# A whole copy of the experts' weights beside their two parts, and one product in place of two for the last 32 tokens

## The chip, the cores and the metric

One core of one Trainium2 chip. The time is the device time of one execution, in microseconds. The kernel before was run three times; the median is 1820.77 us, with 1818.58 and 1825.10 as the ends. Lines (L1254) are lines of the kernel before.

## The reference

The kernel computes one metaformer layer over 64 images of 128 channels and 28 x 28 pixels, in fp32. A first half gates each image by position and by channel. The second half is a mixture of experts over tokens, and the change lies there:

```python
router_probs = jax.nn.softmax(x @ router_w + router_b, axis=-1)
top_p, top_i = jax.lax.top_k(router_probs, K)                  # K = 2 of E = 8 experts
top_p = top_p / jnp.sum(top_p, axis=-1, keepdims=True)
expert_out = jnp.einsum('bnd,edc->bnec', x, expert_w) + expert_b
gathered = jnp.take_along_axis(expert_out, top_i[..., None], axis=2)
return jnp.einsum('bnk,bnkc->bnc', top_p, gathered)
```

Here x is a token's 128 channels after a normalisation, and the result is added to the token.

## The kernel before

**Work and tiles.** Two images make a pair; there are 32 pairs, one after the other. A pair has 1568 tokens: twelve tiles of 128 and a rest of 32. All eight experts are computed for every token, and the gates, 0 for all but two, weigh them. TensorE (PE) multiplies, ACT gates experts 0 to 3 into `part` (`gate_low`, L809), VectorE (DVE) adds experts 4 to 7 (`gate_high`, L1695), GpSimd (POOL) adds the four partial sums into `otok` (`add_token`, L570 and L575).

**The two parts of a number.** The products of the full tiles are made in the faster fp32r form. The centred tokens `cen` are cut into `xh` (rounded, by ACT, `x_high`) and `xl` (what is left, by POOL, `x_low`, L545), the weights into `weh` and `wel`. Three products with 512 columns (L1247 to L1249) make one half of the experts for a tile. The rest of 32 tokens is handled on its own in `rest_products` (L1254): a full fp32 product of `cen` with `weh` and then one with `wel`, each for four pairs of experts. The four write to four groups of 32 rows of one PSUM buffer. Both operands are taken as fp32.

**Where the weights come from.** The experts' weights arrive once by DMA in `raw_we`, a view on the buffer `part`, which is not used for its own purpose before. PE makes their mean, DVE subtracts it in place, ACT copies to `weh`, DVE subtracts that to make `wel`.

**Order.** Each engine runs a list of steps written out by hand. One step takes work of five pairs at different stages; the number behind a call says how many pairs back. On PE the stretch around the changed work is

```python
channels(1, 3)
rstd_turn(1)
logits(4)
low_half(0, 4)        # rest_products
gram_first(3)
router(4)
low_half(1, 4)
gram_turn(3)
finish(3, 5)
channels(2, 3)
joint_c(3)
joint(0, 1, 2)
hidden_c(3)
high_half(1, 4)
```

and later `low_half(2, 4)`, `low_half(3, 4)`, `high_half(3, 4)`. Semaphores tie the engines together: `gram_first` waits for ACT's second group of `chan` (L753), `router` for ACT's copy of the logits (L791), DVE's `route_first` (L1644 to L1658, with `pick` at L1634 to L1637) for `router`, `joint(0, 1)` (L1057) for the PSUM bank that DVE's `finish(3)` (L1705) empties, `high_half(3)` (L1247) for `gate_high(1)` (L1695). ACT and DVE gate by `gv` (L1680), the last step of the routing. POOL's list has `x_low(0)`, `add_token(12)`, `x_low(1)`, `x_low(2)`, `x_low(3)` in this stretch. The DMA queue (SP) stores results, loads images and spreads rows of numbers over all partitions (`y_ch` from `rstd_rows`).

Of the kernel before, what the change touches and what calls it, by code (L numbers as in the profile page):

```python
# [5 lines left out]
ALU = mybir.AluOpType  # L6
ACT = mybir.ActivationFunctionType
F32 = mybir.dt.float32
F32R = mybir.dt.float32r
BF16 = mybir.dt.bfloat16  # L10
AX_X = mybir.AxisListType.X


BATCH, C, HH, WW = 64, 128, 28, 28
S = HH * WW
# [3 lines left out]
E = 8  # L19
PAIR = 2  # L20
# [9 lines left out]
BIG = 1e30  # L30
# [53 lines left out]
TILES = -(-PAIR * S // 128)  # L84
# [27 lines left out]
def metaformer_kernel(nc, a, out):  # L112
    with ExitStack() as ctx:
        def sb(name, shape, dt=F32):
            return ctx.enter_context(nc.sbuf_tensor(name, shape, dt))
# [3 lines left out]
        def sem(name):  # L119
            if name not in sems:  # L120
                sems[name] = ctx.enter_context(nc.semaphore(name))
            return sems[name]
# [30 lines left out]
        pref = sb("pref", [128, E])  # L153
        weh = sb("weh", [C, E, C], F32R)
        wel = sb("wel", [C, E, C], F32R)
        mhalf = sb("mhalf", [128, 2 * NT])


# [2 lines left out]
        cen = sb("cen", [C, PAIR, S])  # L161
# [38 lines left out]
        cg = sb("cg", [C, PAIR])  # L200
        logit = sb("logit", [128, 416])
        lg = sb("lg", [128, TILES, E])
        lg2 = sb("lg2", [128, TILES, E])
        eq = sb("eq", [128, TILES, E])
        first = sb("first", [128, TILES, E])
        second = sb("second", [128, TILES, E])
        mx = sb("mx", [128, 8, TILES])
# [12 lines left out]
        def live(k, p, back):  # L220

            return not isinstance(k, int) or 0 <= 2 * k + p - back < UNITS
# [23 lines left out]
        def need(eng, name, k, p, n, back):  # L246

            if isinstance(k, int) and 2 * k + p - back < 0:
                return
            eng.wait_ge(sem(name), k * (2 * PER[name]) + ((p - back) * PER[name] + n))  # L250

        def rows(i):

            return min(128, PAIR * S - 128 * i)
# [5 lines left out]
        def flat(v):  # L260

            return v[:, :, :].rearrange("p b s -> p (b s)")
# [21 lines left out]
        def bank(use, k, p, back):  # L284

            return rot[((2 * k + p - back + USES[INDEX[use]][1]) * NU + INDEX[use]) % NB]
# [26 lines left out]
        room = part[:, :, :, :].rearrange("p r e c -> p (r e c)")  # L313
# [13 lines left out]
        pad_wc1 = spare[0:DC, 7 * C:10 * C].rearrange("p (t c) -> p t c", t=3)  # L327
        raw_swc1 = scrap[0:DC, 12:13]
        raw_sbc = scrap[:, 13:15]
        raw_we = room[:, 0:E * C].rearrange("p (e c) -> p e c", e=E)  # L330
        avg = scrap[:, 128:256]
        neg_avg = scrap[0:1, 256:384]
        raw_wr = scrap[:, 64:64 + E]
# [563 lines left out]
        def _(pe):  # L897
# [65 lines left out]
            def step(pe, k, p, ahead=False):  # L963
# [285 lines left out]
                    return nc.tensor.matmul(dst[:, :], flat(xl[o])[:, cols_t], hi_w, start=False, stop=True)  # L1249

                def rest_products(dst):
                    for n, w in enumerate((weh, wel)):
                        for g in range(4):
                            last = nc.tensor.matmul(dst[32 * g:32 * g + 32, 0:2 * C], flat(cen)[:, 128 * (TILES - 1):PAIR * S],  # L1254
                                                    w[:, 2 * g:2 * g + 2, :].rearrange("p e c -> p (e c)").bitcast(F32),
                                                    start=(n == 0), stop=(n == 1))
                    return last

                def tile_ready(t, back):
# [4 lines left out]
                def low_half(i, back):  # L1264
                    if live(k, p, back):
                        if opening(k, p, back):
                            pe.wait_ge(sem("weh_ready"), 1)
                            pe.wait_ge(sem("weights_ready"), 1)
                        m, mb = ago(i, 2, back)
                        need(pe, "low_gated", k, p, m + 1, mb)  # L1270
                        if m == 0:
                            need(pe, "high_gated", k, p, 1, mb)
                        dst = low[count_of(k, p, back, i) % 2]
                        if i == 0:
                            need(pe, "centred_ready", k, p, 4, back)
                            rest_products(dst).then_inc(sem("low_filled"), 1)
                        else:
                            tile_ready(tile(i), back)
                            products(dst, tile(i), slice(0, HALF), back).then_inc(sem("low_filled"), 1)
# [108 lines left out]
        def _(dve):  # L1388
# [9 lines left out]
            for e in range(E):  # L1398
                last = nc.vector.memset(pref[:, e:e + 1], float(E - e))
# [77 lines left out]
            def step(dve, k, p, ahead=False):  # L1477
# [5 lines left out]
                def then(ins, name, back):  # L1483

                    count[0] += 1
                    ins.then_inc(sem(name), 1)
                    need(dve, name, k, p, count[0], back)
# [135 lines left out]
                def tiles(v):  # L1623
                    return v.unsqueeze(2).to_broadcast([128, TILES, E])

                def each(v):
                    return v.unsqueeze(1).to_broadcast([128, TILES, E])

                def line(v):
                    return v[:, :, :].rearrange("p i e -> p (i e)")  # L1630

                def pick(logits, top, hot, back):

                    then(nc.vector.tensor_tensor(eq[:, :, :], logits[:, :, :], tiles(top), ALU.is_equal), "route", back)  # L1634
                    then(nc.vector.tensor_tensor(eq[:, :, :], eq[:, :, :], each(pref[:, :]), ALU.mult), "route", back)
                    then(nc.vector.tensor_reduce(mx[:, 4, :], eq[:, :, :], AX_X, ALU.max), "route", back)
                    then(nc.vector.tensor_tensor(hot[:, :, :], eq[:, :, :], tiles(mx[:, 4, :]), ALU.is_equal), "route", back)  # L1637

                def route_first(back):
                    if live(k, p, back):  # L1640
                        count[0] = 0
                        need(dve, "rlogit_filled", k, p, 1, back)
                        src = bank("rlogit", k, p, back)
                        nc.vector.tensor_tensor(lg[:, 0:12, :].rearrange("p (g t) e -> p g t e", t=3),  # L1644
                                                src[:, 0:384].rearrange("p (t g e) -> p g t e", t=3, g=4)[:, :, :, 0:E],
                                                rstd2[:, 0:12].rearrange("p (g t) -> p g t", t=3).unsqueeze(3)
                                                .to_broadcast([128, 4, 3, E]), ALU.mult)
                        n = rows(12)
                        last = nc.vector.tensor_tensor(lg[0:n, 12, :], src[0:n, 480:480 + E],
                                                       rstd2[0:n, 12:13].to_broadcast([n, E]), ALU.mult)  # L1650
                        last.then_inc(sem("rlogit_read"), 1)
                        need(dve, "rlogit_read", k, p, 1, back)
                        then(nc.vector.tensor_reduce(mx[:, 0, :], lg[:, :, :], AX_X, ALU.max), "route", back)
                        pick(lg, mx[:, 0, :], first, back)
                        then(nc.vector.scalar_tensor_tensor(out=line(lg2), in0=line(first), scalar=-BIG, in1=line(lg),
                                                            op0=ALU.mult, op1=ALU.add), "route", back)
                        then(nc.vector.tensor_reduce(mx[:, 1, :], lg2[:, :, :], AX_X, ALU.max), "route", back)
                        nc.vector.tensor_tensor(mx[:, 2, :], mx[:, 1, :], mx[:, 0, :], ALU.subtract)\  # L1658
                            .then_inc(sem("rgap_ready"), 1)
                        assert count[0] == 7  # L1660

                def route_second(back):
                    if live(k, p, back):
                        count[0] = 7
                        pick(lg2, mx[:, 1, :], second, back)
                        assert count[0] == 11

                def route_gates(back):
# [82 lines left out]
                centre_tokens(1, 1)  # L1751
                finish(2, 5)
                route_first(4)
                finish(3, 5)
                route_second(4)
                route_gates(4)
                normalise(0, 0, 1)
# [46 lines left out]
```

## Time and profile before

| | |
|---|---|
| three runs, median (ends) | 1820.77 us (1818.58 to 1825.10) |
| the profiled execution, its time | 1818.09 us |
| its span, first to last instruction | 1816.3 us |
| mean granted TensorE clock | 0.99 |
| busy, share of the span | PE 96%, DVE 79%, ACT 67%, POOL 62% |
| one pair in steady work, from first rest product to the next pair's | 53.4 to 53.7 us |
| L1254 | 512 records of PE |

A record of PE is one pass of a matmul; an fp32 product has two, so that eight products for a pair are 16 records. The timeline merges successive instructions of one kind into one row, with the start of the first and the time until the end of the last. Ends of matmuls are modelled, since they overlap: starts are the surer numbers. An idle time stands in brackets, with what ended it.

### The profile page before, as it was taken

The numbers are of one execution on the slowest core, as the hardware profiler recorded it, in microseconds if no ns is written. First come the engines' busy times: TensorE is split into PE (matmuls) and PEld (weight loads), VectorE is DVE, ScalarE is ACT, GpSimd is POOL, SyncE is SP. The second block draws the span as 40 slices with busy tenths as digits, with TensorE's granted clock in tenths as the row PEclk, the third lists the DMA queues.
The fourth block names the chain that finished last, engine by engine and source line by source line (L and its number), as shares of the span: only waits on it lengthen the run. The fifth ranks groups of instructions, "written<-read, shape, count | busy, mean of one in ns | idle before, by whom it ended". The sixth has DMA issues, their size and how long they took to land.

```text
span 1816.3 us, 39474 instructions
## 1 busy us (share of the span) xinstructions
PE 1748.9 (96%) x13396; PEld 1295.2 (71%) x13396; DVE 1434.1 (79%) x4703; ACT 1210.0 (67%) x3346; POOL 1132.6 (62%) x1268
## 2 busy tenths in 40 slices
PE   4789999999999999999999999999999999999996
PEld 2467777777777777777777777777777777777774
DVE  4467888888888888888888888888888888887666
ACT  4447667677666667666767776666776676776554
POOL 1135666766667676666767666767666676766565
PEclk9799999999999999999999999999999999999998
DMA  4122222112222211222211222221122221121111
GB/s 136 37 73 72 73 90 75 70 63 82 73 90 90 73 64 63 90 72 90 83 62 64 81 73 90 90 73 63 64 90 72 90 90 60 62 78 65 44 55 54
DMA packets 56181, 135.18 MB, mean 74 GB/s; under 512 B 16268, under 2 KB 18333, under 8 KB 55982
## 3 DMA queue, kind: packets, MB, share of 16 engines
q1 hardware_dynamic: 55320, 130.81, 20.8%
q8 instruction: 110, 1.80, 0.4%
q10 hardware_dynamic: 662, 1.84, 0.4%
q14 instruction: 89, 0.73, 0.1%
HBM read 106.50 MB, written 26.13 MB: 73 GB/s over the span
## 4 chain that ended last, share of the span: by engine, by line
PE 92%; DVE 3%; ACT 2%; DMA 1%; issue 1%; POOL 1%; SPq 0%; POOLq 0%; ACTq 0%; DVEq 0%
PE rot L1101 6%; PE rot L1111 6%; PE rot L1102 6%; PE low L1247 5%; PE high L1247 5%; PE rot L1057 5%; PE low L1249 5%; PE low L1248 5%; PE high L1249 5%; PE high L1248 5%; PE rot L1037 4%; PE rot L1070 3%; PE rot L1238 3%; PE rot L981 3%; PE rot L1004 3%; PE rot L1200 3%
## 5 line engine op out<-in xcount | busy, mean ns | idle before, releaser
L809 ACT ACTIVATE part<-low,gv 128x128 f32<-128x128 f32 (+1 forms) x1664 | 475.2, 376 | 166.9 <-PE low L1249 89.4
L570 POOL TENSOR_TENSOR part<-part 128x256 f32<-128x256 f32 (+1 forms) x416 | 331.4, 797 | 327.3 <-DVE part L1695 321.5
L1695 DVE SCALAR_TENSOR_TENSOR part<-high,gv,part 128x128 f32<-128x128 f32 x1536 | 424.7, 342 | 81.3 <-ACT part L809 47.7
L575 POOL TENSOR_TENSOR otok<-part 128x128 f32<-128x128 f32 (+1 forms) x416 | 263.5, 633 | 32.6
L1101 PE MATMUL rot<-x1h,wch 128*128 128x256 f32 x960 | 237.3, 286 | 0.0
L1102 PE MATMUL rot<-x1h,wcl 128*128 128x256 f32 x960 | 230.9, 280 | 0.0
L535 POOL TENSOR_TENSOR tp_l<-tp,tp_h 128x448 fp32r<-128x448 f32 x64 | 65.6, 1024 | 239.4 <-ACT tp_h L686 239.3
L1101 PEld LDWEIGHTS rot<-x1h,wch 128*128 128x128 f32 x960 | 181.4, 189 | 3.5 <-issue 0.9
L1102 PEld LDWEIGHTS rot<-x1h,wcl 128*128 128x128 f32 x960 | 181.9, 189 | 1.3
L1247 PE MATMUL low<-weh,xh 128*128 128x512 f32 x384 | 170.2, 443 | 7.8 <-DVE part L1695 7.5
L703 ACT ACTIVATE j<-rot,bggs 128x448 f32<-128x448 f32 (+3 forms) x256 | 136.1, 582 | 58.5 <-PE rot L1057 55.6
L1247 PE MATMUL high<-weh,xh 128*128 128x512 f32 x384 | 163.7, 426 | 2.7 <-DVE part L1695 2.6
L1249 PE MATMUL low<-weh,xl 128*128 128x512 f32 x384 | 152.1, 396 | 0.0
L1249 PE MATMUL high<-weh,xl 128*128 128x512 f32 x384 | 151.8, 395 | 0.0
L1248 PE MATMUL low<-wel,xh 128*128 128x512 f32 x384 | 151.7, 395 | 0.0
L1248 PE MATMUL high<-wel,xh 128*128 128x512 f32 x384 | 151.1, 394 | 0.0
L554 POOL TENSOR_TENSOR x1l<-tok,x1h 128x1024 fp32r<-128x1024 f32 x64 | 117.7, 1838 | 33.6 <-ACT x1h L741 32.7
L1111 PE MATMUL rot<-x1l,wch 128*128 128x256 f32 x960 | 137.6, 279 | 0.5 <-POOL x1h L559 0.5
L545 POOL TENSOR_TENSOR xl<-cen,xh 128x384 fp32r<-128x384 f32 x128 | 127.1, 1015 | 2.7 <-ACT xh L786 2.7
L1111 PEld LDWEIGHTS rot<-x1l,wch 128*128 128x128 f32 x960 | 125.4, 189 | 3.2 <-POOL x1h L559 0.7
L753 ACT ACTIVATE chan<-rot,bc 128x256 f32<-128x256 f32 x160 | 68.7, 470 | 69.2 <-PE rot L1113 69.1
L1644 DVE TENSOR_TENSOR lg<-rot,rstd 128x96 f32<-128x96 f32 x32 | 8.2, 258 | 132.7 <-PE rot L1228 132.7
(247 smaller groups left out, 3995.3 us busy)
## 6 DMA issues: line engine op xcount, KB each, us to landing
xin<-in_x SPq DMA_DIRECT2D x32, 784.0 KB, 4.4
x<-in_x SPq DMA_DIRECT2D x32, 784.0 KB, 4.3
cen<-shift_rows SPq DMA_DIRECT2D x32, 784.0 KB, 4.0
out<-x SPq DMA_DIRECT2D x64, 392.0 KB, 2.4
y_ch<-rstd_rows SPq DMA_DIRECT2D x32, 768.0 KB, 3.8
otok<-in_ggs_w SPq DMA_DIRECT2D x1, 600.2 KB
tok<-in_ggs_w SPq DMA_DIRECT2D x1, 600.2 KB
rstd_rows<-both_rows SPq DMA_DIRECT2D x32, 7.0 KB
```

What stands on the lines that cost most here:

```text
L545: nc.gpsimd.tensor_tensor(flat(xl[o])[:, own], flat(cen)[:, own], flat(xh[o])[:, own].bitcast(F32), ALU.subtract)\
L570: nc.gpsimd.tensor_tensor(part[0:n, slot, 0:2, :], part[0:n, slot, 0:2, :], part[0:n, slot, 2:4, :], ALU.add).then_inc(sem("half_sum"), 1)
L575: nc.gpsimd.tensor_tensor(otok[0:n, t, :], part[0:n, slot, 0, :], part[0:n, slot, 1, :], ALU.add).then_inc(sem("token_ready"), 1)
L703: nc.scalar.activation((j1, j2)[m][0:rows, b, cols(q)], bank(f"joint{b}{q}{m}", k, p, back)[0:rows, 0:width(q)], ACT.Relu, bias=bggs[0:row ...
L809: last = nc.scalar.activation(part[0:n, turn % RING, e, :], src, ACT.Copy, scale=gv[par(p, back)][0:n, t, e:e + 1])
L1101: nc.tensor.matmul(dst, wch[:, j, rows], hi_x, start=(j == 0), stop=False)
L1102: nc.tensor.matmul(dst, wcl[:, j, rows], hi_x, start=False, stop=False)
L1111: nc.tensor.matmul(dst, wch[:, j, rows], x1l[:, j, :, :].rearrange("p b c -> p (b c)"), start=False, stop=False)
L1247: nc.tensor.matmul(dst[:, :], flat(xh[o])[:, cols_t], hi_w, start=True, stop=False)
L1248: nc.tensor.matmul(dst[:, :], flat(xh[o])[:, cols_t], lo_w, start=False, stop=False)
L1249: return nc.tensor.matmul(dst[:, :], flat(xl[o])[:, cols_t], hi_w, start=False, stop=True)
L1695: last = nc.vector.scalar_tensor_tensor(out=own, in0=src, scalar=gv[par(p, back)][0:n, t, HALF + e:HALF + e + 1], in1=own, op0=ALU.mult, o ...
```

## The change

The whole weights get a buffer of their own, `we`, and stay there after the two parts are made. The rest of 32 tokens takes one full fp32 product with `we` for each pair of experts, where it took one with `weh` and one with `wel`. To make room, `lg2`, the router's logits with the first choice masked out, is given up, and the masked logits are written over `lg`. `raw_we` becomes another name for `we`; the lines that load, centre and cut the weights are the same.

```diff
         wel = sb("wel", [C, E, C], F32R)
+        we = sb("we", [C, E, C])
...
-        lg2 = sb("lg2", [128, TILES, E])
...
-        raw_we = room[:, 0:E * C].rearrange("p (e c) -> p e c", e=E)
+        raw_we = we[:, :, :]
...
                 def rest_products(dst):
-                    for n, w in enumerate((weh, wel)):
-                        for g in range(4):
-                            last = nc.tensor.matmul(dst[32 * g:32 * g + 32, 0:2 * C], flat(cen)[:, 128 * (TILES - 1):PAIR * S],
-                                                    w[:, 2 * g:2 * g + 2, :].rearrange("p e c -> p (e c)").bitcast(F32),
-                                                    start=(n == 0), stop=(n == 1))
+                    for g in range(4):
+                        last = nc.tensor.matmul(dst[32 * g:32 * g + 32, 0:2 * C], flat(cen)[:, 128 * (TILES - 1):PAIR * S],
+                                                we[:, 2 * g:2 * g + 2, :].rearrange("p e c -> p (e c)"), start=True, stop=True)
                     return last
...
-                        then(nc.vector.scalar_tensor_tensor(out=line(lg2), in0=line(first), scalar=-BIG, in1=line(lg),
+                        then(nc.vector.scalar_tensor_tensor(out=line(lg), in0=line(first), scalar=-BIG, in1=line(lg),
                                                             op0=ALU.mult, op1=ALU.add), "route", back)
-                        then(nc.vector.tensor_reduce(mx[:, 1, :], lg2[:, :, :], AX_X, ALU.max), "route", back)
+                        then(nc.vector.tensor_reduce(mx[:, 1, :], lg[:, :, :], AX_X, ALU.max), "route", back)
...
-                        pick(lg2, mx[:, 1, :], second, back)
+                        pick(lg, mx[:, 1, :], second, back)
```

## Rows read from the trace of the kernel before

**Rows 1.** Busy us (instructions) of each engine in a stretch, clock, DMA share, GB/s.
```profile
900.00:1200.00 300.00, 300.00 (x2318) 221.50 (x2317) 250.07 (x825) 212.97 (x590) 197.11 (x219) 1.00 0.22 77
```
**Rows 2.** Timeline of PE, pair at 943.6: start, us, engine, line, what, count.
```profile
943.56 0.61 PE L1254 MATMUL low<-weh,cen 128*32 128x256 f32 x8
944.00 0.61 PE L1254 MATMUL low<-wel,cen 128*32 128x256 f32 x8
944.54 1.16 PE L1145 MATMUL rot<-chan 128*128 128x128 f32 x8
945.53 0.60 PE L1228 MATMUL rot<-ident,logit 128*128 128x128 f32 x4
```
**Rows 3.** Line L1254: count, ns least/median/most, first and last start.
```profile
L1254 PE MATMUL low<-wel,cen x256: 379/379/634, 141.4 to 1779.7; 128*32 128x256 f32 x128
```
**Rows 4.** Timeline of ACT, pair at 943.6.
```profile
942.84 0.84 ACT L753 ACTIVATE chan<-rot,bc 128x256 f32<-128x256 f32 x2 [1.55 <-PE rot L1113]
...
943.81 0.51 ACT L791 COPY logit<-rot 128x416 f32<-128x416 f32 x1
```
**Rows 5.** Timeline of DVE, pair at 997.0.
```profile
1000.24 0.72 DVE L1634 TENSOR_TENSOR eq<-lg,mx 128x104 f32<-128x104 f32 x1
1001.00 0.96 DVE L1635 TENSOR_TENSOR eq<-eq,pref 128x104 f32<-128x104 f32 x1
...
1002.28 0.27 DVE L1637 TENSOR_TENSOR first<-eq,mx 128x104 f32<-128x104 f32 x1
...
1003.27 0.58 DVE L1705 TENSOR_TENSOR x<-rot,x 128x416 f32<-128x416 f32 x1
```
**Rows 6.** Timeline of POOL, pair at 997.0: second and third `x_low` of the row.
```profile
999.83 1.01 POOL L545 TENSOR_TENSOR xl<-cen,xh 128x384 fp32r<-128x384 f32 x1
...
1000.79 1.04 POOL L545 TENSOR_TENSOR xl<-cen,xh 128x384 fp32r<-128x384 f32 x1
```
**Rows 7.** Timeline of DVE, pair at 943.6.
```profile
946.82 0.58 DVE L1634 TENSOR_TENSOR eq<-lg,mx 128x104 f32<-128x104 f32 x1
...
949.72 0.58 DVE L1705 TENSOR_TENSOR x<-rot,x 128x416 f32<-128x416 f32 x1
```
**Rows 8.** Timeline of POOL, pair at 943.6: the `x_low` in the middle.
```profile
946.28 1.00 POOL L545 TENSOR_TENSOR xl<-cen,xh 128x384 fp32r<-128x384 f32 x1
```
**Rows 9.** Timeline of DVE, pair at 836.5.
```profile
839.73 0.40 DVE L1634 TENSOR_TENSOR eq<-lg,mx 128x104 f32<-128x104 f32 x1
...
841.44 0.67 DVE L1637 TENSOR_TENSOR first<-eq,mx 128x104 f32<-128x104 f32 x1
```
**Rows 10.** Timeline of POOL, pair at 836.5: three `x_low` back to back.
```profile
838.99 3.00 POOL L545 TENSOR_TENSOR xl<-cen,xh 128x384 fp32r<-128x384 f32 x3
```
**Rows 11.** Timeline of DVE, moments of the pair behind, at 932.8.
```profile
932.78 0.18 DVE L1496 TENSOR_TENSOR sm<-st 128x14 f32<-128x14 f32 x1
932.88 0.73 DVE L1497 TENSOR_TENSOR sm<-st 128x14 f32<-128x14 f32 x1
```
**Rows 12.** Timeline of POOL at the same time.
```profile
932.77 0.79 POOL L570 TENSOR_TENSOR part<-part 128x256 f32<-128x256 f32 x1
```
**Rows 13.** Timeline of PE: `joint(0,1)` of two pairs, `high_half(3)` of one.
```profile
950.48 0.42 PE L1057 MATMUL rot<-tp_h,mix_h 64*68 64x448 f32 x2
...
1003.83 0.49 PE L1057 MATMUL rot<-tp_h,mix_h 64*68 64x448 f32 x2
...
1011.51 0.39 PE L1247 MATMUL high<-weh,xh 128*128 128x512 f32 x1
```
**Rows 14.** Timeline of DVE, pair at 997.0: `gate_high(1)`.
```profile
1010.05 1.12 DVE L1695 SCALAR_TENSOR_TENSOR part<-high,gv,part 128x128 f32<-128x128 f32 x4
```
**Rows 15.** Timeline of PE, last pair: `low_half(2)`.
```profile
1790.99 0.77 PE L1247 MATMUL low<-weh,xh 128*128 128x512 f32 x1 [6.39 <-DVE part L1695]
```
**Rows 16.** Waits of all engines: who for whom, us in all, times, longest.
```profile
DVE y_ch L1525 <- DMA y_ch<-rstd_rows: 15.0, 2, 10.6
```

## Prediction

> **What bounds the kernel now.** I read the busy time by stretch first. In 300 us of steady work TensorE (PE) is busy for all 300, VectorE (DVE) for 250, ACT for 213, GpSimd (POOL) for 197, at full clock [rows 1]. So PE sets the pace, and PE time that goes should come back as time, unless something released by another engine is late. The timeline of PE round the changed line comes second, for the price; the timelines of DVE, POOL and ACT behind it come third, for what is late next. The reader is to see that PE never stands idle for long, but that twice in each pair of images it arrives less than 0.1 us behind DVE. That makes this a question of margins.
>
> **What goes.** Per pair, four fp32 products with `weh` (16 records of PE in all for both weights) start at 943.56, four with `wel` at 944.00, and the next work at 944.54 [rows 2]. One set of four, with its weight loads, is a step of 0.44 us (0.43 by the unrounded starts; 0.54 is the step that includes the change to other work, and it stays). The line has 256 records for `wel`, two for each product, 379 ns almost everywhere, from the first pair to the last [rows 3]: 32 pairs. Were nothing else to wait, the change is worth 32 x 0.43 = 13.8 us.
>
> **What is added or moved.** `we` is another tensor that receives the same DMA as before and is centred by the same instructions; the ACT copy and the DVE subtraction that make `weh` and `wel` are unchanged, once each. No queue gets or loses a transfer. The routing writes its masked logits back into `lg` in place of `lg2`: same instruction, same shape, on an engine that runs in order, so 0. The tensors behind `we` lie 4 KB further on per partition; no row shows a price for a place, and I take 0 both ways. The work that begins 0.43 earlier is the real edit.
>
> **Who meets PE early.** Four things begin before the removed step and are needed behind it. (a) `gram_first` needs ACT's chan copies, which end at 943.68 [rows 4]; PE would come at 944.11. Free. (b) The router's transposes need the logit copy, ended 944.32 [rows 4]; PE would come at 945.10. Free. (c) The spread rstd rows: DVE waited for that transfer twice in the whole run, at most 10.6 us, both at the start [rows 16]. Free. (d) POOL's `x_low`, three instructions back to back, not released by PE here. DVE's routing starts when PE's router transposes end, so it moves 0.43 earlier, and POOL's three do not. These two engines block each other, and here the gain is decided.
>
> In the pair at 997 (call it kind 1) DVE starts L1634 at 1000.24 and takes 0.72, L1635 takes 0.96, and the later L1637 0.27 [rows 5]; undisturbed each takes 0.27. POOL's instructions end at 1000.84 and 1001.83 [rows 6], and DVE's two end 0.12 and 0.13 after them. So a DVE instruction with two SBUF inputs waits out the POOL instruction in flight, and gets in between two. The end of the routing hangs on POOL's third `x_low`, not on PE. Behind it come `finish(3)` (L1705), for which PE waits in `joint(0,1)` (L1057), the gates, and `gate_high(1)` (L1695), for which PE waits in `high_half(3)`. Margins: L1705 ends at 1003.85 [rows 5] and PE is at L1057 from 1003.83 [rows 13], none; L1695 ends at 1011.17 [rows 14], and PE starts 0.34 later [rows 13], about what its release takes. If DVE does not come earlier, PE gains nothing here.
>
> Does it? **Kind 1**: L1634 would come at 999.81. POOL's second `x_low` starts at 999.83 [rows 6]. Rows show the edge elsewhere: L1496 started 0.01 after a POOL instruction and ran its normal 0.18; L1497, 0.11 after the same start, was held, 0.73 [rows 11, 12]. So 0.02 ahead should get in. Then L1635 waits for the second `x_low` instead of the third, L1637 for the third, and it ends near 1001.95 in place of 1002.55: 0.60 earlier, or 0.33 if POOL is meanwhile put off by one DVE instruction (0.27). The bounds of the edge are 0 (missed) and 0.60; I take the hit, being nearer to the row of L1496, and at least 0.43 of it. PE then gains its 0.43 and some 0.02 of today's waits: 0.45. By the length of L1634 and whether L1637 is held, 14 of the 32 pairs are of this kind.
> **Kind 2** (the pair at 943.6; 8 of 32): L1634 starts at 946.82, takes 0.58; POOL's instruction runs from 946.28 [rows 7, 8]. It would come at 946.39, 0.11 after POOL's start, like the L1497 that was held. DVE ends when it did. L1705 ends at 950.30 [rows 7], PE was at L1057 at 950.48 [rows 13] and would be at 950.05: it waits until some 950.35, so 0.13 stays.
> **Kind 3** (the pair at 836; 6 of 32): POOL runs from 838.99 for 3.00, and L1637 too is held, until 842.11, 0.12 behind the last `x_low` [rows 9, 10]. Coming 0.43 earlier changes none of these ends: 0.
> The other four: in the first pair and in the one at 1692 DVE is not held: 0.43 each. In the last two PE waits for DVE anyway (6.39 us in the last, [rows 15]) and DVE would run into POOL: 0.
>
> Sum: 14 x 0.45 + 8 x 0.13 + 6 x 0 + 2 x 0.43 = 6.3 + 1.0 + 0.9 = **8.2 us**. The profiled execution took 1818.1 (span 1816.3), so 1809.9; the median of the runs shown is 1820.8, 2.7 above it, and I forecast against that: **1812.5 us**.
>
> The Trainium skill ("SBUF — State Buffer", section "Who interferes with whom") says that a DVE instruction with two SBUF inputs contends with a GpSimd instruction that reads SBUF, and that whoever issues first keeps the port for its whole instruction. The rows of kind 1 to 3 agree, except that L1496, 0.01 late, was not held. By the strict rule the sum stays 8.2 as long as L1634 is the first by those 0.02 us, and is 1.9 if it is not.
>
> **Rivals.**
> (1) Full gain. The kinds are not fixed: each pair of kind 2 or 3 is followed by one of kind 1. If kind 1 settles in, every pair gives 0.43: 13.8 us, 1807. The distances of successive pairs scatter from 53.4 to 53.7 (table of the profile); if they all came to the lower end, 0.1 or so per pair would be added, 3 us: 1804. For it: PE's 300 of 300. Against: the missing margin at L1057.
> (2) Nothing to speak of. The edge at 999.83 is missed: kind 1 gives 0, the sum is 8 x 0.13 + 2 x 0.43 = 1.9, 1819. For it: 0.02 us is a margin that a small shift of POOL's instructions undoes. It is also what remains if DVE's next instructions are held one POOL instruction longer. That eight products stay is excluded: the loop over the two parts is gone.
> (3) Slower. An earlier DVE instruction that gets in holds POOL back (POOL's L570 took 0.79 in [rows 12] beside DVE). If the third `x_low` ends later by one DVE instruction, 0.27, the routing ends later, and PE, with no margin at L1057, loses 0.27 against today in each of 28 pairs: 7.6 us, 1828. It decides from the point where L1705 ends more than about 0.1 us after PE's present arrival at L1057. Against it: POOL held by 0.27 would have to come with no DVE gain.
>
> **Numbers.** Forecast (gain 5.5 to 11 us) 0.42; full gain (more than 11) 0.28; nothing (within 5.5 us either way) 0.23; slower 0.07. A measurement here can tell some 0.3%, 5.5 us, from no change. Faster 0.70, same 0.23, slower 0.07. The range goes from just under the lower end of (1), 1803.5, to the time of (2) with half a microsecond, 1819.5; the forecast alone would have 1810 to 1815.
>
> **What would show it.** The changed line has 256 records of PE, none with `wel`, and the step from the last logit product to `gram_first` falls from 0.98 to 0.55: price right. The router's transposes follow the first rest product after 1.54, not 1.97 [rows 2]. L1634 of 0.27 where it was 0.72: the edge was hit; of 1.0: missed. If L1705 ends less than 0.1 before the second product of `joint(0,1)` in most pairs, PE's time went into that wait. Wrong I am if kinds other than these turn up, if PE shows new waits before `gram_first` or the router, or if the distance between pairs falls by 0.43 everywhere: then the margins did not matter.

## The result, and the profile after

The changed kernel takes 1818.68 us (median of 20 runs, 1815.81 to 1822.48), the kernel before 1822.66 in 20 runs on the same chip (1818.42 to 1825.10). The ratio is 0.9981, 95% interval 0.9973 to 0.9989: some 3.5 us faster (2.0 to 4.9), where 8.2 were forecast. It is less than the 0.3% that the prediction set as what can be told from no change. The profiled execution took 1818.96.

The work that was to go has gone, at its price. First the source line of the rest products in the trace of after (count, ns least/median/most, first and last start), then PE's timeline in the pair that begins at 945.5 (a pair is named by the start of its first logits, L1218):

```profile
L1253 PE MATMUL low<-we,cen x256: 379/379/634, 145.1 to 1780.8; 128*32 128x256 f32 x128
```
```profile
945.50 0.91 PE L1218 MATMUL rot<-cen,wr 128*32 128x416 f32 x8
946.22 0.61 PE L1253 MATMUL low<-we,cen 128*32 128x256 f32 x8
946.77 1.16 PE L1145 MATMUL rot<-chan 128*128 128x128 f32 x8
947.76 0.60 PE L1228 MATMUL rot<-ident,logit 128*128 128x128 f32 x4
...
952.65 0.77 PE L1057 MATMUL rot<-tp_h,mix_h 64*68 64x448 f32 x2
```

256 records in place of 512 [rows 3]. `gram_first` (L1145) stands 0.55 behind the first rest product and the router's transposes (L1228) 1.54; they stood 0.98 and 1.97 behind it [rows 2]. So PE is 0.43 us earlier at the router in each pair. But the row of L1057 covers 0.77 us for two records, where it was 0.42 [rows 13]: the second of them, which needs the PSUM bank that `finish(3)` empties, waits. Records merge in that view; where the wait is long enough the trace breaks them, as in the pair at 998.8, and names DVE's `finish(3)` (L1703 now, L1705 before; lines behind the change have numbers smaller by two):

```profile
1005.95 0.42 PE L1057 MATMUL rot<-tp_h,mix_h 64*68 64x448 f32 x1
1006.63 0.42 PE L1057 MATMUL rot<-tp_h,mix_h 64*68 64x448 f32 x1 [0.26 <-DVE x L1703]
```

DVE's routing in a pair that was to be of kind 1, at 1213.0. First DVE, then POOL's second and third `x_low` of the row, both of after:

```profile
1216.57 1.09 DVE L1632 TENSOR_TENSOR eq<-lg,mx 128x104 f32<-128x104 f32 x1
1217.69 0.97 DVE L1633 TENSOR_TENSOR eq<-eq,pref 128x104 f32<-128x104 f32 x1
1218.69 0.26 DVE L1634 TENSOR_REDUCE mx<-eq 128x13 f32<-128x104 f32 x1
1218.99 0.27 DVE L1635 TENSOR_TENSOR first<-eq,mx 128x104 f32<-128x104 f32 x1
...
1219.98 0.58 DVE L1703 TENSOR_TENSOR x<-rot,x 128x416 f32<-128x416 f32 x1
```
```profile
1216.54 0.99 POOL L545 TENSOR_TENSOR xl<-cen,xh 128x384 fp32r<-128x384 f32 x1
...
1217.50 1.04 POOL L545 TENSOR_TENSOR xl<-cen,xh 128x384 fp32r<-128x384 f32 x1
```

The first step of `pick` (L1632 now) starts at 1216.57, 0.03 behind POOL's `x_low` at 1216.54, and takes 1.09: held to the end of that instruction, and the next one for 0.97 to the end of the one behind it. In the pair at 997 before, the same two took 0.72 and 0.96 [rows 5]. DVE came 0.43 earlier and was held 0.38 longer, so that `finish(3)` starts 6.96 us behind the pair's first logits (1213.02), before 7.02 (1003.27 [rows 5] less that pair's 996.25). The table of groups says it for the whole run (after; its busy time and mean ns):

```profile
L1632 DVE TENSOR_TENSOR eq<-lg,mx 128x104 f32<-128x104 f32 x64 | 37.4, 585 | 1.1
```
and the same of before:
```profile
L1634 DVE TENSOR_TENSOR eq<-lg,mx 128x104 f32<-128x104 f32 x64 | 26.7, 417 | 1.1
```

These are 10.7 us more in 64 instructions that do the same work. On the page of after DVE is busy for 1445.2 us (1434.1 before), and the chain that ended last passes more through it:

```profile
PE 1747.8 (96%) x13140; PEld 1287.8 (71%) x13140; DVE 1445.2 (80%) x4703; ACT 1206.8 (66%) x3346; POOL 1131.4 (62%) x1268
PE 88%; DVE 7%; ACT 2%; issue 1%; DMA 1%; POOL 1%; SPq 0%; POOLq 0%; ACTq 0%; DVEq 0%
```

Before, that chain had 92% PE and 3% DVE. PE is busy for 1.1 us less of the run, not 13.8: a wait that the modelled ends of the records cover is no idle time there, such as that of the second record of L1057, which starts at 953.00 where the first is shown until 953.07.

**Distance between pairs.** The time from one pair's first logits (L1218) to the next's is the measure used from here on, since what lies ahead of the first pair moved by 4 us between the two profiled executions (first logits at 140.2 before and 144.4 after), whatever the change. From the third pair to the 29th, 26 distances, PE's timeline of after:

```profile
250.17 0.91 PE L1218 MATMUL rot<-cen,wr 128*32 128x416 f32 x8
...
1640.66 0.91 PE L1218 MATMUL rot<-cen,wr 128*32 128x416 f32 x8
```
and of before:
```profile
246.55 0.91 PE L1218 MATMUL rot<-cen,wr 128*32 128x416 f32 x8
...
1638.77 0.91 PE L1218 MATMUL rot<-cen,wr 128*32 128x416 f32 x8
```

1390.49 / 26 = 53.48 and 1392.22 / 26 = 53.55: the change is worth 0.07 us for a pair, where PE's work is 0.43 shorter. With the first two and the last four pairs it makes 3.3 us (1676.1 from first logits to end before, 1672.8 after), which is the measured difference.

### The profile page after: what moved, and what is told of

Read it like the earlier page. It is cut to its first block, busy times and chain, and to the rows that moved or that the text cites. A ratio compares the mean times of both kernels' runs of the same rounds, so it can differ in the third digit from the quotient of the medians.

```text
span 1817.2 us, 38962 instructions
## 1 busy us (share of the span) xinstructions
PE 1747.8 (96%) x13140; PEld 1287.8 (71%) x13140; DVE 1445.2 (80%) x4703; ACT 1206.8 (66%) x3346; POOL 1131.4 (62%) x1268
## 4 chain that ended last, share of the span: by engine, by line
PE 88%; DVE 7%; ACT 2%; issue 1%; DMA 1%; POOL 1%; SPq 0%; POOLq 0%; ACTq 0%; DVEq 0%
PE rot L1101 6%; PE rot L1111 5%; PE rot L1102 5%; PE rot L1057 5%; PE high L1247 5%; PE low L1247 5%; PE high L1249 5%; PE high L1248 5%; PE low L1249 5%; PE low L1248 4%; PE rot L1037 4%; PE rot L1070 3%; PE rot L981 3%; PE rot L1004 3%; PE rot L1200 3%; PE rot L971 2%
## 5 line engine op out<-in xcount | busy, mean ns | idle before, releaser
L570 POOL TENSOR_TENSOR part<-part 128x256 f32<-128x256 f32 (+1 forms) x416 | 328.6, 790 | 324.8 <-DVE part L1693 319.0
L1247 PE MATMUL low<-weh,xh 128*128 128x512 f32 x384 | 169.8, 442 | 8.5 <-DVE part L1693 8.2
L1247 PE MATMUL high<-weh,xh 128*128 128x512 f32 x384 | 163.7, 426 | 2.7 <-DVE part L1693 2.6
L517 POOL TENSOR_TENSOR rstd<-var,mhalf 128x14 f32<-128x14 f32 x32 | 91.1, 2846 | 25.4 <-DVE var L1502 25.2
```

The costliest lines, as they stand in the source:

```text
L570: nc.gpsimd.tensor_tensor(part[0:n, slot, 0:2, :], part[0:n, slot, 0:2, :], part[0:n, slot, 2:4, :], ALU.add).then_inc(sem("half_sum"), 1)
L1247: nc.tensor.matmul(dst[:, :], flat(xh[o])[:, cols_t], hi_w, start=True, stop=False)
```

## Experiments

Two theories stood after the result. **The lock**: DVE's routing is earlier by 0.43, but POOL's two last `x_low` hold it, so `finish(3)` ends when it did, and PE, now early, waits for its bank. **The rival**: the change brings a cost of its own (the place of `we`, the routing writing over `lg`), or the eight products were never worth 0.43 because something hid them. Each line is the median time, the ratio to the kernel before measured beside it, its 95% interval and the mean distance, as above (53.55 before, 53.48 after).

| kernel | us | ratio | distance |
|---|---|---|---|
| a_router | 1821.25 | 0.9991 (0.9980 to 1.0002) | 53.49 |
| b_router | 1834.97 | 1.0073 (1.0059 to 1.0088) | 53.96 |
| a_xlow | 1810.41 | 0.9933 (0.9919 to 0.9948) | 53.04 |
| b_xlow | 1821.55 | 0.9994 (0.9983 to 1.0006) | 53.48 |
| a_two | 1821.35 | 1.0004 (0.9995 to 1.0012) | 53.55 |
| a_nudge | 1812.46 | 0.9961 (0.9946 to 0.9975) | 53.33 |
| a_xlow3 | 1807.20 | 0.9924 (0.9911 to 0.9937) | 53.08 |
| a_banks | 1814.53 | 0.9967 (0.9954 to 0.9979) | 53.28 |
| b_xlow3 | 1821.25 | 0.9996 (0.9985 to 1.0008) | 53.50 |
| b_banks | 1823.40 | 1.0009 (0.9996 to 1.0022) | 53.56 |
| a_xlow3_banks | 1810.03 | 0.9931 (0.9914 to 0.9948) | 53.12 |

a_ kernels are made from the changed kernel, b_ from the one before.

### The routing out of the lock: a_xlow, b_xlow

```diff
                 x_low(1, 4)
-                x_low(2, 4)
-                x_low(3, 4)
                 add_token(0, 4)
 ...
                 add_token(4, 4)
+                x_low(2, 4)
+                x_low(3, 4)
```

> The changed kernel with POOL's x_low(2) and x_low(3) moved behind add_token(4), away from DVE's routing; PE's order is untouched. Theory: L1634, L1635 and L1637 take 0.27 us each except where x_low(1) meets the first, L1705 ends well before PE reaches joint(0,1), distance about 53.0 us, ratio 0.992, if the later xl and token sums make no wait of their own. Rival: as before the move, ratio 0.997 to 0.999.

> The kernel before with the same move of x_low(2) and x_low(3). Theory: distance of pairs about 53.4 us, ratio 0.998, so that the difference to the changed kernel with this move is the price of the products, 0.43 us a pair, some 12 us. Rival: the difference is some 3 us.

Measured: 0.9933, as expected, and 0.9994, where 0.998 was expected. In a_xlow only `x_low(1)` can still meet the routing (in nine pairs it holds the first step, for 0.83 to 0.95 us in all, which costs nothing). In the pair at 992.5 nothing of POOL lies beside it, and DVE's timeline reads

```profile
996.07 0.27 DVE L1632 TENSOR_TENSOR eq<-lg,mx 128x104 f32<-128x104 f32 x1
996.37 0.27 DVE L1633 TENSOR_TENSOR eq<-eq,pref 128x104 f32<-128x104 f32 x1
...
997.96 0.58 DVE L1703 TENSOR_TENSOR x<-rot,x 128x416 f32<-128x416 f32 x1
```

The same instructions take 0.27 in place of 1.09 and 0.97. Between the two kernels, which differ by the whole change, lie 0.43 us for each pair (53.48 - 53.04): its full price. The same move on the kernel before is worth 0.07. There the routing ended about when PE needed it, so the hold cost next to nothing; the change made the hold the bound.

### One move is enough: a_xlow3, b_xlow3

Only `x_low(3)` is moved behind `add_token(4)`.

> The changed kernel with only POOL's x_low(3) moved behind add_token(4). Theory: L1634 is still held by x_low(2), to about 4.6 us behind the logits, but L1635 and L1637 are free; L1705 ends at about 6.5, before PE reaches joint(0,1) at 7.13, so that the whole price comes back: distance 53.0 us, ratio 0.993, as with both moved. Rival (it is the sum of what POOL takes from DVE, so that half the move gives half): distance 53.25, ratio 0.996.

> The kernel before (eight products, lg2) with only POOL's last x_low of the row moved behind the additions to the tokens. Theory (before the change DVE's held routing ended about when PE needed it, so PE was the bound and freeing DVE is worth next to nothing; the change makes PE earlier, and only then does the hold cost): ratio to the kernel before 0.998 to 1.001, mean distance between pairs 53.45 to 53.55 us, and the same edit on the changed kernel is 0.7% ahead of it, 0.43 us for each pair. Rival (the moved x_low is worth its 0.4% on any kernel, and the eight products fewer are worth only 0.2% beside it): ratio 0.995 to 0.996, distance near 53.25.

Measured: 0.9924 and 0.9996, distances 0.41 apart. DVE, POOL (its `x_low(1)` and `x_low(2)` in one row) and PE of a_xlow3, pair at 992.3:

```profile
995.82 1.10 DVE L1632 TENSOR_TENSOR eq<-lg,mx 128x104 f32<-128x104 f32 x1
996.95 0.27 DVE L1633 TENSOR_TENSOR eq<-eq,pref 128x104 f32<-128x104 f32 x1
...
998.54 0.58 DVE L1703 TENSOR_TENSOR x<-rot,x 128x416 f32<-128x416 f32 x1
```
```profile
994.83 1.97 POOL L545 TENSOR_TENSOR xl<-cen,xh 128x384 fp32r<-128x384 f32 x2
```
```profile
999.40 0.42 PE L1057 MATMUL rot<-tp_h,mix_h 64*68 64x448 f32 x2
```

The first step is still held, for 1.10, to 0.12 behind POOL's end at 996.80; the second no longer is. `finish(3)` ends at 999.12, before PE comes to L1057 at 999.40, and the two records of L1057 take 0.42 as before. It is the third `x_low`, and not the hold of the first step, that costs the gain. This is the lowest ratio found, 0.76% ahead of the kernel before; its interval overlaps with those of a_xlow and a_xlow3_banks.

### Later by a tenth on POOL: a_nudge

A tiny instruction of POOL (99 ns, a memory set of a buffer that nothing reads then) is put ahead of `x_low(1)`, so that POOL comes later and DVE first. The line that names its semaphore is left out here.

```diff
                 add_token(12, 5)
+                if live(k, p, 4):
+                    need(pool, "pad_set", k, p, 1, 5)
+                    nc.gpsimd.memset(valid[:, :], 0.0).then_inc(sem("pad_set"), 1)
                 x_low(1, 4)
```

> The changed kernel with one tiny added POOL instruction (a memset of the 128x1 tile valid, which is no longer needed then) ahead of x_low(1), so that POOL's three x_low start a little later, by perhaps 0.1 to 0.3 us. Theory: L1634, which now comes 0.02 to 0.13 us after the start of x_low(2) and is held for 1.1 us, comes while x_low(1) still runs and gets in ahead of x_low(2); L1635 and L1637 are then held by x_low(2) and x_low(3), the routing ends 0.3 to 0.6 us sooner, and the distance falls from 53.48 by 0.1 to 0.35 us: more POOL work, yet 3 to 9 us faster than the changed kernel, ratio 0.993 to 0.997 against before. Rival (the x_low delay PE or DVE by their length, not by where they start): the distance grows or stays, ratio 0.998 or more.

Measured: 0.9961, by the ratios 3.6 us faster than the changed kernel, with an instruction more in each pair; the two intervals touch, but the distance fell from 53.48 to 53.33. Its lines stand three lower. POOL and DVE in the pair at 994.2:

```profile
996.73 0.10 POOL L598 MEMSET valid<- 128x1 f32 x1
...
997.75 1.12 POOL L545 TENSOR_TENSOR xl<-cen,xh 128x384 fp32r<-128x384 f32 x1
```
```profile
997.74 0.27 DVE L1635 TENSOR_TENSOR eq<-lg,mx 128x104 f32<-128x104 f32 x1
998.04 0.95 DVE L1636 TENSOR_TENSOR eq<-eq,pref 128x104 f32<-128x104 f32 x1
...
999.33 0.67 DVE L1638 TENSOR_TENSOR first<-eq,mx 128x104 f32<-128x104 f32 x1
...
1000.72 0.58 DVE L1706 TENSOR_TENSOR x<-rot,x 128x416 f32<-128x416 f32 x1
```

This is kind 1 as the prediction had it: DVE, 0.016 ahead of the second `x_low`, takes 0.27 and stretches it to 1.12; the next step waits for the second and not the third, the later one for the third. From this pair's first logits to the next's are 53.15 us, 0.46 less than the 53.61 of kind 1 before, and 0.45 was the forecast for a hit. The added instruction does not do this everywhere. Where the second `x_low` started 0.09 or more ahead of DVE, the hold stayed; three pairs that took 53.56 to 53.59 in after (357.3, 891.9, 1213.0) now have POOL's row later by 0.8 and take 53.80 to 53.84, while two of 53.80 take 53.15. What is measured is the balance.

### The bank: a_banks, b_banks, a_xlow3_banks

The second product of `joint(0, 1)` takes the bank that ACT's channel copies free, and not the one of `finish(3)`; ACT's `router_exp` moves behind `joint_c(3)`.

```diff
-    ("fin3", 5, "out_ready", 4),
     ("chan2", 3, "chan_ready", 3),
+    ("fin3", 5, "out_ready", 4),
 ...
-                router_exp(4)
                 channels(2, 3)
                 joint_c(3)
+                router_exp(4)
```

> The changed kernel in which joint(0,1) no longer waits for DVE: fin3 and chan2 change places in the rotation of PSUM banks, and ACT does router_exp behind joint_c. POOL's list is untouched, so the routing stays late. Theory: the wait at the second product of joint(0,1) goes, but PE meets the same lateness at low_half(2) or high_half(3), whose gates hang on gate_high(1): distance 53.4 to 53.5 us, ratio 0.997 to 0.998, hardly better than the change alone. Rival (the bank is the whole reason): distance 53.0 us, ratio 0.993.

> The kernel before with the two PSUM banks exchanged, so that the second product of joint(0, 1) takes the bank that ACT's channel copies free and not the one that finish(3) frees. Theory (before the change no wait for finish(3) stood there): ratio 0.999 to 1.001, distance 53.5 to 53.6 us. Rival (the exchange was worth its 0.2% by itself): ratio 0.997 to 0.998, distance near 53.35.

> The changed kernel with both edits: last x_low moved and banks exchanged. Theory (both edits remove the same wait of PE, the one for finish(3), so the second finds nothing left): as with the moved x_low alone, ratio 0.991 to 0.994, distance 53.05 to 53.15 us. Rival (two different losses, which add up): ratio 0.989 to 0.990, distance near 52.9.

Measured: 0.9967, 1.0009 and 0.9931. The ratio of a_banks is close to what the theory had (0.997 to 0.998), but its distance of 53.28 lies below the 53.4 to 53.5 of the theory and above the 53.0 of the rival: the bank is more than half of the loss, not all. PE of a_banks, pair at 945.6:

```profile
952.70 0.49 PE L1057 MATMUL rot<-tp_h,mix_h 64*68 64x448 f32 x2
```

The wait at L1057 is gone (0.49 for two records, 0.77 in after), which shows that it was the wait for `finish(3)`. But only part of the price comes back: 0.20 us a pair more than in after, 0.27 of 0.43 in all. A routing that ends late is then waited for further on: DVE's `gate_high(1)` and PE's `high_half(3)` behind it, in the pair at 892.3 of a_banks:

```profile
906.87 0.34 DVE L1693 SCALAR_TENSOR_TENSOR part<-high,gv,part 128x128 f32<-128x128 f32 x1
```
```profile
906.91 0.39 PE L1249 MATMUL low<-weh,xl 128*128 128x512 f32 x1
907.26 0.50 PE L1247 MATMUL high<-weh,xh 128*128 128x512 f32 x1
```

PE starts 0.05 behind the end of the gate, where it had been 0.34 before [rows 13, 14]. The step to it is 0.35 and its first record 0.50; in after the same step is 0.23 and the record 0.39. So 0.23 us are lost here when the bank doesn't bind first. From the third pair to the 28th it is so in 20 of 26, and the mean over the 26 is 0.15, which is what is missing of the 0.43. On the kernel before the exchange is worth nothing, and beside the moved `x_low` it adds nothing either (0.9931 and 0.9924, intervals overlapping): both remove the same loss.

### What the change itself costs: a_two

The changed kernel with its buffer and its writing over `lg`, but the eight products with `weh` and `wel` put back.

```diff
-                    for g in range(4):
+                    for n, w in enumerate((weh, wel)):
+                        for g in range(4):
 ...
-                                                we[:, 2 * g:2 * g + 2, :].rearrange("p e c -> p (e c)"), start=True, stop=True)
+                                                    w[:, 2 * g:2 * g + 2, :].rearrange("p e c -> p (e c)").bitcast(F32),
+                                                    start=(n == 0), stop=(n == 1))
```

> The changed kernel with the rest's two products put back (weh and wel, eight products), while we keeps its own buffer and the masked logits are still written over lg. Both theories of the wait expect the time of the kernel before, ratio 1.000 within 0.001, distance of pairs 53.5 to 53.6 us. If the new buffer or the write over lg cost something that hid a gain, it shows here as a ratio above 1.001, up to the 10 us that are missing (1.005).

Measured: 1.0004 (0.9995 to 1.0012), distance 53.55. The buffer and the reuse cost nothing that can be seen; the rival falls.

### The router first: a_router, b_router

```diff
                 logits(4)
-                low_half(0, 4)
                 gram_first(3)
                 router(4)
+                low_half(0, 4)
```

> The changed kernel with the rest's product moved on PE behind gram_first and router, so that the router's transposes come 0.54 us sooner behind the logits. Theory (the routing on DVE ends with POOL's last x_low, and PE waits for it at joint(0,1)): DVE's first pick starts 0.54 earlier, gets in one x_low earlier, L1637 ends about 0.6 earlier, the wait at the second product of joint(0,1) (0.35 us and more in every pair of the changed kernel) goes, and the distance of pairs falls from 53.48 to about 53.0 us: some 15 us under the kernel before, ratio 0.992. Rival (the 0.43 us are given back at some other wait, so that DVE's routing is not what holds PE): distance stays near 53.4 to 53.5, ratio 0.997 to 0.999.

> The kernel before with the same move of the rest's eight products behind gram_first and router. Theory: DVE starts 0.98 us sooner, the small waits at joint(0,1) go, the distance of pairs falls from 53.55 to 53.4 us, some 4 us in all, ratio 0.998; the difference to the same move in the changed kernel is then the products' price, 0.43 us a pair, some 12 us. Rival: the difference between the two is some 3 us, as between the kernels without the move.

Measured: 0.9991 and 1.0073, where the theory had 0.992 and 0.998: both missed. DVE's routing starts earlier and the wait at L1057 is gone (0.42 for its two records at 952.10), as hoped, but no time is won. PE of a_router, and ACT's copies of `chan` at the same time:

```profile
944.50 0.91 PE L1218 MATMUL rot<-cen,wr 128*32 128x416 f32 x8
945.48 1.13 PE L1145 MATMUL rot<-chan 128*128 128x128 f32 x8
946.45 0.60 PE L1228 MATMUL rot<-ident,logit 128*128 128x128 f32 x4
946.98 0.64 PE L1253 MATMUL low<-we,cen 128*32 128x256 f32 x8
947.55 0.50 PE L1247 MATMUL low<-weh,xh 128*128 128x512 f32 x1
```
```profile
944.50 0.84 ACT L753 ACTIVATE chan<-rot,bc 128x256 f32<-128x256 f32 x2 [1.56 <-PE rot L1113]
```

From L1218 to L1247 are 3.05 us for the same records that took 2.62 in after (945.50 to 948.12, where L1247 starts). The move gives back on PE what it gains on DVE. Two steps are longer. From L1218 to L1145 it is 0.98, where the next work behind L1218 came after 0.72 in after: `gram_first` needs the second copy of `chan`, which ends at 945.34, 0.84 behind the first logits, as it does in every trace here (0.83 or 0.84). The rest products had stood in front of it and hidden that. And from L1228 to the rest products it is 0.53, where it was 0.36 from L1228 to L1247. What holds is the difference of the two: 53.96 - 53.49 = 0.47 for a pair, again the price of the four products where DVE is in time.

## Why the prediction was wrong

**What bounds, the price, what is added: right.** The set of four products costs 0.43 (0.98 to 0.55 in the steps of PE; 0.43, 0.41 and 0.47 between the kernels of three pairs of experiments). The new buffer and the reuse of `lg` cost 0 (a_two). `gram_first` and the router's transposes were free, as said in (a) and (b); (a) holds only while the rest products stand in front of `gram_first`, as a_router shows.

**The mechanism: right.** The gain was decided between DVE and POOL, in the routing, and PE's freed time went into the wait at L1057 (a_xlow3 against b_xlow3).

**Kind 1: the step that failed**, "I take the hit". The first step of `pick` was to come 0.02 us ahead of the second `x_low`. In after it starts, in the 11 pairs that stand like kind 1, from 0.004 ahead to 0.041 behind, and is held every time: 1.08 to 1.13 us. POOL's second `x_low` starts some 0.04 nearer to the pair's first logits than before (3.51 to 3.56 behind them, 3.55 to 3.58 in all but one such pair before), and a margin of half that was the whole of 14 x 0.45 = 6.3 us. The distance of the pairs that were and stayed of kind 1 fell from some 53.61 to some 53.57, not by 0.45; all 14 together gave 0.3 us. The size for a hit was right (0.46 in a_nudge); the bet was on a tie of two hundredths, POOL's start was treated as fixed to that, and the row that the hit was argued from, L1496, is no such tie (last section). Rival (2) named this mechanism and its sum of 1.9 us, 1819. The measured 3.5 (2.0 to 4.9) is nearest to it, but not all of it comes from what rival (2) adds up.

The Trainium skill ("SBUF — State Buffer", section "Who interferes with whom") calls the port pair that DVE and GpSimd share an exclusive lock, and says that the order of issue decides who blocks. In nine of the 11 pairs the trace agrees: POOL starts first and DVE waits. In two DVE is shown 0.003 and 0.004 ahead and is held all the same. By that rule, once the 0.02 are missed, the sum was 1.9.

**Kind 2: right.** 0.13 was forecast; seven of the eight pairs go from 53.41 to 53.30. The eighth became kind 3 and lost 0.11.

**Kind 3: 0 was forecast, and its six pairs gave 1.0 us.** The one that stayed kind 3 gave nothing, as said. But in four of them POOL's row starts 0.8 us earlier against the logits in after (2.46 behind them for the first `x_low`, 3.24 to 3.26 before), so that they stand like kind 2 and gave 0.2 each; the fifth gave 0.24. On the other side four pairs of kind 1 became kind 3: three of them take 53.80 in place of 53.61 (the pair at 998.8 with its 0.26 of wait is one), and the fourth, at 571.7, had DVE first and gave 0.46. The sum took each pair's kind as fixed. What moves POOL's row from pair to pair is not shown. It need not be the change: in a_two, whose PE work is that of before, all six pairs are of another kind than before too, and the mean distance is the same.

**The other four.** First pair and the one at 1692: 0.35 and 0.53, forecast 0.43 each. The last two gave 0.22 and 0.24 where 0 was forecast. In all 0.3 (kind 1), 0.6 (kind 2), 1.0 (kind 3) and 1.3 make the 3.3 of the trace. That the time came out near rival (2) with its 1.9 is thus in part luck.

**`high_half(3)` was misread.** The prediction took the 0.34 between `gate_high(1)` and PE's start there for release time, so that no margin was left. In a_banks PE follows the gate by 0.05. So some 0.29 of the 0.34 was margin: the bank at L1057 binds first, and the gate becomes the next wait once the bank is free. The sum doesn't change by this, since the first of the two decides.

**Rival (1)**, full gain, needed the routing out of the lock, and comes true in a_xlow and a_xlow3 (1807.2 for the latter; 1807 was its time). **Rival (3)**, slower: where the first step of `pick` gets in just ahead it does stretch POOL, by 0.08 to 0.14, but not by the 0.27 supposed, and `finish(3)` came earlier all the same (6.53 behind the logits in a_nudge, 6.96 in after).

## What to carry to other kernels

When PE is full and the instructions behind another engine's result have no slack, a cut on PE is worth what the other engine lets through: look for what holds that engine (here a run of POOL instructions that nobody waits for) and move it in the same change. The two edits were worth 0.2% and nothing each alone, and 0.76% together, so try an enabling move on both kernels before it is called useless. Where a forecast rests on who comes first by two hundredths of a microsecond, give both outcomes even chances, since POOL's start against PE scatters by more than that from pair to pair.

## What was not expected of the hardware

**The tie between DVE and POOL is sharp, and can be read.** For all DVE instructions `eq<-lg,mx` (two SBUF inputs) and POOL's `x_low` in the traces of all kernels here, the start of DVE less that of POOL, and what became of DVE:

```
DVE start less POOL start    ran at once (0.27)    held (1.0 to 1.1)
-52 to -14 ns                25                    0
 -5 to  +2 ns                 4                    17
+11 to +138 ns                0                    83
```

Where DVE ran, the POOL instruction took 1.08 to 1.15 in place of 0.98 to 1.02. A held one ends 0.12 behind POOL's shown end. L1496 (by the lines of before), which [rows 11, 12] show unhurt 0.01 behind a POOL start, had been the row that the hit was argued from; no `eq<-lg,mx` at +11 ns or more behaves like it. The traces say what that row is: in all 13 of them L1496 starts 1 to 44 ns behind POOL's L570, 28 times in each, and runs at once in 363 of 364 cases. It directly follows another DVE instruction, L1495, which started some 0.09 before it and so ahead of POOL. So it is not a late comer that got in, but the next of a DVE chain that was there first; L1497, 0.09 to 0.13 behind the same POOL start, was held in 268 of 363 cases. Why the second of the chain always passes and the third only sometimes is not shown.

**More work on POOL made the kernel faster**: 99 ns more in each pair, 3.6 us less in all (a_nudge).

**With the router first PE needs 0.43 more for the same records, and more than one thing is in it.** The way from the logits to the first 128x512 product is 2.62 in after and 3.05 in a_router; b_router too is 0.41 longer a pair than before. 0.26 of it lie ahead of `gram_first`. PE reaches it 0.98 behind the first logits (0.99 in five pairs) in 27 pairs of each of the two kernels, and ACT's copy that it needs ends at 0.84. PE could have been there after 0.72, or 0.82 if a step from 128*32 to 128*128 tiles costs the 0.10 that it costs behind L1254 (0.54 against 0.44 [rows 2]). So an estimate of 0.16 to 0.26 is a wait for ACT. The profile names no releaser there, and no run took the wait away. The other 0.17 lie between the router's transposes and the rest products, where the tiles change from 128*128 to 128*32; whether that change is the cause was only argued.
